# A two-layer transformer tower on one core: the first weight on ScalarE's queue, and small operations, weight turns and final products in another order

## The chip, the cores and the metric

The kernel runs on 1 core of one Trainium2 chip. The metric is the device time of an execution in microseconds (us), the median of several runs.

## The reference

From each of 64 rows of 375 numbers, four overlapping patches of 128 (stride 64) are cut: 256 tokens of 512 features.

```
h = patches @ W.T + b                                # 64 x 4 patches -> 512
h = h + attention0(layernorm(h))                     # 16 heads of 32, over the 4 positions
h = h + experts(layernorm(h))                        # 16 experts of 192, the two best of each token
h = h + attention1(layernorm(h))                     # causal, 16 heads, 4 key/value heads
h = h + ffn1(layernorm(h))                           # 512 -> 2048 -> 512
attention0: activations rounded to 8 bits per token or head, weights to {-1, 0, 1} * mean|W|
ffn1:  x = fwht(x * SU_ug) / 64
       x = silu(x @ W_gate.T * s_g) * (x @ W_up.T * s_u)
       x = fwht(x * SU_dp) / 64
       x = x @ W_down.T * (Wscale_dp * 64)
```

fwht is the Walsh-Hadamard transform over the last axis. Wscale_dp scales each of the 512 output features.

## The kernel before

The 256 tokens lie as two tiles of 128 partitions (`TILES`, index t), and the whole tower runs on them without leaving the core's memory. The program for each engine is written out by hand, in order, and the engines meet only at counting semaphores (`wait_ge`, `then_inc`). An instruction that waits holds up all that stands behind it on its engine. So the order of the lines is the schedule.

**Precision.** Products that need it are done as three: high part by high part, high by low, low by high. ScalarE casts the high part (`main_high`, `rest_high`, `f_high`, `xt_high`, `wd_high`, `u_high`), VectorE subtracts for the low one (`main_low` L1424, `rest_low` L1428, `f_low`, `xt_low`, `wd_low`, `u_low`), TensorE multiplies. Matmuls of plain fp32 take two passes.

**Opening.** SyncE issues every load. The first are the bias row, the patches, the patch weight `tok_w`, then the four weights of the first attention, 1 MB each, into `big_raw` (L373). TensorE makes the embedding (L778). ScalarE sums |W| of a weight (`abs_sum`, L449); TensorE adds that sum over the partitions (`weight_total`, L784); VectorE makes thresholds of it (`weight_scale`, L1202 to L1205); ScalarE turns the weight into two sign matrices (`side`, L460). TensorE multiplies the rounded, transposed tokens (`quantised_transposes` L800) by them (`project`, L790) for queries, keys and values, m = 0, 1, 2. VectorE takes each head's largest value (`largest`, L1264), its scale (`floors`, L1270 and L1272, `head_factors`, `head_steps`) and the rounded heads (`head_round`). `key_products`, a fold, the softmax, and the products with the values follow on VectorE; TensorE sums the latter (L853). Between these, TensorE runs products that nobody reads: `early_warm` (L757) and `warm_up`/`keep_warm` (L750).

**Turns.** The rows of W_down in `down_raw` have to be Hadamard-transformed too. `fold_step` does a part on VectorE; the rest is 16 `turn`s: TensorE multiplies a chunk into a bank (L767, two passes), ScalarE copies it back (`turned_back`, L476). Turns 0 to 7 stand in the first attention, turns 8 to 15 (`TURNS_FIRST` is 8) around the second. `TURN_BANK` says which bank each uses.

**Experts.** 32 units (expert by tile) of three parts each of four products (`unit_products`, L883), one bank of four in turn; `hidden` (L1453) makes silu(gate) * up; `dn` (L723 to L725) multiplies by the down weights of a pair of experts.

**Second attention.** `keys_and_values`, `queries_high`, `queries_low`, `swapped`, then on VectorE `products`, `weights`, `weighted_values`; TensorE sums with `values` (L1027) and multiplies by the output weight.

**Last feed-forward.** 16 chunks f: `ffn_gu(f)` (L1101, L1118), and from f = 7 on `down(f - 7)` behind it. `down(c)` adds chunk c for both tiles to banks 2 and 6. Chunks 12 to 15 are done for tile 0 first, then for tile 1. VectorE multiplies each finished tile by `wsdp` (Wscale_dp; L1790), adds h (L1792), and SyncE stores it in two halves (L412).

## Time and profile before

| | |
|---|---|
| median of 3 runs | 281.83 us (281.79 to 283.18) |
| the profiled execution's own time | 282.39 us |
| its span, first to last instruction | 280.6 us |
| TensorE, matmuls | 264.8 us, 94% of the span |
| VectorE | 227.1 us, 81% |
| ScalarE | 149.4 us, 53% |
| granted TensorE clock, mean | 0.996 |

A matmul's busy time overlaps the next one's, so TensorE at 94% is not TensorE at its peak. A row of the timeline gives start, duration, engine, line, operation, and in brackets how long the engine had been idle before it and what ended that. x4 says that four like instructions were put together. SPq is SyncE's DMA queue.

### The profile page before, as it was taken

How to read it: one execution, taken by the hardware profiler on the slowest of the kernel's cores; microseconds unless marked ns; L12 is line 12 of the kernel's file. 1: busy time of each engine (PE TensorE's matmuls, PEld its weight loads, DVE VectorE, ACT ScalarE, POOL GpSimd, SP SyncE). 2: the span in 40 equal slices, each digit the busy share in tenths (PEclk: the TensorE clock that was granted, in tenths of full speed). 3: DMA queues.
4: the chain of work that ended last, by engine and by line, in shares of the span. 5: the costliest groups of instructions: out<-in, count | busy, mean ns of one | idle time of the engine just before them, and what ended most of it. 6: DMA issues, size and time to landing. Idle time of an engine off the chain costs nothing. (4 is left out here: it accounts for less than half of the span.)

```text
span 280.6 us, 3960 instructions
## 1 busy us (share of the span) xinstructions
PE 264.8 (94%) x1477; PEld 217.6 (78%) x1480; DVE 227.1 (81%) x409; ACT 149.4 (53%) x234; POOL 6.3 (2%) x19
## 2 busy tenths in 40 slices
PE   8779789989999999999999999999999999999993
PEld 3445454658899999989999897766689989999872
DVE  1969999897999988889898676888958894878783
ACT  2798772345563565655555524535466662653530
POOL 0200000000000000000000000000100000000000
PEclk9999999999999999999999999999999999999998
DMA  6960899904244808172630068095000000000003
GB/s 229 427 250 2 290 378 411 446 12 139 86 159 181 306 33 336 23 316 74 262 110 6 0 224 374 2 363 238 0 0 2 0 2 0 0 2 0 2 2 75
DMA packets 6997, 40.43 MB, mean 144 GB/s; under 512 B 1217, under 2 KB 1473, under 8 KB 5314
## 3 DMA queue, kind: packets, MB, share of 16 engines
q1 hardware_dynamic: 6978, 40.18, 37.6%
q8 instruction: 12, 0.20, 0.3%
q14 instruction: 7, 0.06, 0.1%
HBM read 39.13 MB, written 0.52 MB: 141 GB/s over the span
## 5 line engine op out<-in xcount | busy, mean ns | idle before, releaser
L1101 PE MATMUL bank<-s_xf_hi,s_f_hi 128*128 128x256 f32 x128 | 31.2, 282 | 0.5 <-ACT s_xf_hi L675 0.5
L1101 PE MATMUL bank<-s_xf_hi,s_f_lo 128*128 128x256 f32 x128 | 31.1, 281 | 0.0
L543 ACT ACTIVATE s_silu<-bank 128x192 f32<-128x192 f32 x32 | 10.5, 331 | 36.6 <-PE bank L883 32.6
L883 PE MATMUL bank<-s_w_hi,s_xt_hi 128*128 128x384 f32 (+1 forms) x128 | 29.3, 350 | 0.6 <-DVE s_h L1417 0.6
L883 PE MATMUL bank<-s_w_lo,s_xt_hi 128*128 128x384 f32 (+1 forms) x128 | 27.9, 339 | 0.3 <-DVE s_w_lo L1431 0.3
L883 PE MATMUL bank<-s_w_hi,s_xt_lo 128*128 128x384 f32 (+1 forms) x128 | 27.7, 338 | 0.3 <-DVE s_xt_lo L1194 0.3
L1101 PEld LDWEIGHTS bank<-s_xf_hi,s_f_hi 128*128 128x128 f32 x128 | 24.1, 188 | 1.1 <-issue 0.7
L1625 DVE TENSOR_TENSOR s_f_lo<-s_ffn_raw,s_f_hi 128x1024 fp32r<-128x1024 f32 x16 | 19.6, 1225 | 6.0 <-ACT s_f_hi L622 5.9
L1101 PEld LDWEIGHTS bank<-s_xf_hi,s_f_lo 128*128 128x128 f32 x128 | 24.1, 188 | 0.4
L883 PEld LDWEIGHTS bank<-s_w_hi,s_xt_hi 128*128 128x128 f32 x128 | 21.9, 188 | 2.2 <-DVE s_h L1417 0.8
L883 PEld LDWEIGHTS bank<-s_w_lo,s_xt_hi 128*128 128x128 f32 x128 | 22.8, 188 | 0.7 <-DVE s_w_lo L1431 0.7
L883 PEld LDWEIGHTS bank<-s_w_hi,s_xt_lo 128*128 128x128 f32 x128 | 22.8, 188 | 0.5 <-DVE s_xt_lo L1194 0.5
L697 ACT ACTIVATE s_fs<-bank,s_cols 128x256 f32<-128x256 f32 x16 | 7.6, 475 | 26.0 <-PE bank L1118 26.0
L1426 DVE TENSOR_TENSOR s_w_lo<-s_moe_raw,s_w_hi 128x1024 fp32r<-128x1024 f32 x15 | 18.3, 1223 | 3.1 <-ACT s_w_hi L482 3.1
L723 PE MATMUL bank<-s_dn_hi,s_ht_hi 128*128 128x512 f32 x48 | 19.3, 403 | 0.0
L725 PE MATMUL bank<-s_dn_hi,s_ht_lo 128*128 128x512 f32 x48 | 18.8, 392 | 0.0
L724 PE MATMUL bank<-s_dn_lo,s_ht_hi 128*128 128x512 f32 x48 | 18.8, 392 | 0.0
L1118 PE MATMUL bank<-s_xf_lo,s_f_hi 128*128 128x256 f32 x128 | 17.8, 282 | 0.0
L482 ACT CAST s_w_hi<-s_moe_raw 128x1024 fp32r<-128x1024 f32 x16 | 16.7, 1047 | 1.9 <-PE bank L883 1.8
L767 PE MATMUL bank<-s_big_raw,s_con 128*128 128x512 f32 x32 | 15.7, 602 | 1.7 <-DMA s_big_raw<-down_w 1.7
L622 ACT CAST s_f_hi<-s_ffn_raw 128x1024 fp32r<-128x1024 f32 x16 | 16.8, 1050 | 0.2
L1118 PEld LDWEIGHTS bank<-s_xf_lo,s_f_hi 128*128 128x128 f32 x128 | 16.3, 188 | 0.0
(235 smaller groups left out, 559.7 us busy)
## 6 DMA issues: line engine op xcount, KB each, us to landing
s_moe_raw<-moe_gu SPq DMA_DIRECT2D x16, 768.0 KB, 7.2
s_ffn_raw<-ffn_w SPq DMA_DIRECT2D x4, 2048.0 KB, 10.9
s_moe_raw<-moe_dn SPq DMA_DIRECT2D x8, 768.0 KB, 4.4
s_big_raw<-att_w SPq DMA_DIRECT2D x4, 1024.0 KB, 8.9
s_big_raw<-down_w SPq DMA_DIRECT2D x4, 1024.0 KB, 8.0
s_l_raw<-l_w SPq DMA_DIRECT2D x1, 2560.0 KB, 21.1
out<-s_h SPq DMA_DIRECT2D x4, 128.0 KB, 2.3
s_tok_w<-tok_w SPq DMA_DIRECT2D x1, 256.0 KB, 2.6
```

The source lines that it names most:

```text
L482: act.copy(main_part("w_hi", e), main_of(e)).then_inc(guh_ready, 1)
L543: act.activation(B["silu"][i % 2][:], unit_bank(i)[:, 0:F], ACT.Silu).then_inc(silu_done, 1)
L622: act.copy(M["w_hi"][f % 2][:], ffn_chunk_raw(f)).then_inc(fwh_ready, 1)
L723: pe.matmul(dst, x_hi, w_hi, start=first, stop=False)
L724: pe.matmul(dst, x_hi, w_lo, start=False, stop=False)
L725: return pe.matmul(dst, x_lo, w_hi, start=False, stop=last)
L767: pe.matmul(bank[TURN_BANK[i]][:], con[:, K_H:K_H + P], down_raw[:, TURNS[i], :], start=True, stop=True).then_inc(turn_done, 1)
L883: ins = pe.matmul(unit_bank(i)[:, 0:n], xt(k, t)[part % 2], w[:, k, 0:n], start=(first and k == 0), stop=(last and k == KC - 1))
L1101: pe.matmul(tb(j, n)[:, 0:TOK], M[w][j][:, k, n * P:(n + 1) * P], M["xf_hi"][:, k, :], start=(w == "w_hi" and k == 0), stop=False)
L1118: last = pe.matmul(tb(j, n)[:, 0:TOK], M["w_hi"][j][:, k, n * P:(n + 1) * P], M["xf_lo"][:, k, :], start=False, stop=(k == KC - 1))
L1426: dve.tensor_tensor(main_part("w_lo", e), main_of(e), main_part("w_hi", e).bitcast(F32), ALU.subtract)
L1625: dve.tensor_tensor(M["w_lo"][f % 2][:], ffn_chunk_raw(f), M["w_hi"][f % 2][:].bitcast(F32), ALU.subtract).then_inc(fw_ready, 1)
```

## The change

1. **First weight.** `big_raw` for m = 0 is loaded by ScalarE's queue, as its first instruction, and no longer by SyncE's.
2. **First attention.** The five `early_warm(6)` between and behind the projections are gone (30 products), `WARM[0]` is 12 in place of 18. `weight_total(2)` stands between the two `project(0, ., 1)`. On VectorE `floors` of each projection and `weight_scale(2)` stand one wait earlier, the scaling of `sh[:, 5]` is done by ScalarE, and `weight_scale(3)` stands behind the second `key_products`.
3. **Way into the experts.** `rest_low(0)` stands where tile 0's projection is finished, `keep_warm(bank[5], 4)` is gone, unit 0's parts run as 0, 2, 1, and the first part of unit 2 runs before unit 1.
4. **Last expert pair and second attention.** `last_dn` does the four products with the high hidden part first and then the two with the low one. `turn(8)` moves from before them to before `keys_and_values(1)`; turns 9 to 11 stand together before `values(1)`, 12 to 14 before `scaled_transposes(1, ...)`, 15 right before the last feed-forward. `queries_low(0)` stands before `transposes(5)`. ScalarE's and VectorE's counterparts move accordingly.
5. **Last feed-forward.** `down(7)` and `down(8)` run after all 16 `ffn_gu`. The rows of chunks 12 to 15 of W_down are multiplied by `wsdp` on VectorE after f = 7, 8, 11 and 12; these chunks are added up in banks 3 and 7. The sum of chunks 0 to 11 is multiplied by `wsdp` and added to h while TensorE is at the last four, whose sum is then only added. The second half of each stored tile goes by ScalarE's queue.

```diff
-        WARM, GAP, FILL = (18, 24), 20, 7
+        WARM, GAP, FILL = (12, 24), 20, 7
-        TURN_BANK = (3, 7, 5, 3, 7, 3, 7, 3, 5, 1, 5, 1, 5, 0, 4, 0)
+        TURN_BANK = (3, 7, 5, 3, 7, 3, 7, 3, 5, 1, 5, 1, 0, 4, 0, 4)
@@ sync
-            for m in range(4):
+            for m in range(1, 4):
...
             for t in range(TILES):
                 sp.wait_ge(out_ready, t + 1)
-                for j in range(2):
-                    sp.dma_start(by_pos[2 * t + j], h[j * HALF:(j + 1) * HALF, t, :]).then_inc(stored, 16)
+                sp.dma_start(by_pos[2 * t], h[0:HALF, t, :]).then_inc(stored, 16)
@@ scalar
+            act.dma_start(big_raw[:, 0:KC * C], att_w[0]).then_inc(ld_att[0], 16)
...
+            act.wait_ge(g_ready, 1)
+            act.activation(A["sh"][:, 5], A["g3"][:, 0], ACT.Copy, scale=float(D) ** -0.5).then_inc(gx_ready, 1)
...
             f_high(0)
+            q_out(0)
             xt_high(5)
-            q_out(0)
             act.activation(spare1[:], neg_half[:], ACT.Exp)
+            exp(2, L["sc"][:, 2, 0, 0:2], L["sc"][:, 3, 0, 0:2])
             q_out(1)
-            exp(2, L["sc"][:, 2, 0, 0:2], L["sc"][:, 3, 0, 0:2])
+            turned_back(8)
             kv_out(1)
-            turned_back(9)
-            turned_back(10)
...
+                if c >= FC - 4:
+                    act.wait_ge(rows_scaled, c - FC + 5)
...
+            for t in range(TILES):
+                act.wait_ge(out_ready, t + 1)
+                act.dma_start(by_pos[2 * t + 1], h[HALF:P, t, :]).then_inc(stored, 16)
@@ tensor
             project(0, 0, 1)
+            weight_total(2, bank[3][:, 0:1])
             project(0, 1, 1)
-            weight_total(2, bank[3][:, 0:1])
-            early_warm(6, bank[1])
...
+            pe.wait_ge(gu_ready, 1)
             unit_products(0, 0, True, False)
-            keep_warm(bank[5], 4)
+            unit_products(0, 2, False, False)
             pe.wait_ge(xt_ready, 3)
-            unit_products(0, 1, False, False)
+            unit_products(0, 1, False, True)
...
+            unit_products(2, 0, True, False)
             pe.wait_ge(xt_hi_ready, 4)
...
             transposes(4, L["xn"], 0)
-            turn(8)
-            dn(PAIRS - 1, 1, 1, 3)
+            last_dn()
...
             queries_low(1)
+            turn(8)
             keys_and_values(1)
             swapped(1)
...
-            turn(9)
-            turn(10)
             values(0)
...
-            turn(11)
-            turn(12)
+            for i in (9, 10, 11):
+                turn(i)
             values(1)
...
-            for i in range(13, 16):
+            for i in range(12, 15):
                 turn(i)
...
                 lane_transform(j, xt_lo, False).then_inc(xf_done, 1)
+            turn(15)
...
             for f in range(FC):
                 ffn_gu(f)
-                if f >= 7:
+                if 7 <= f < FC - 2:
                     down(f - 7)
-            for c in range(9, FC - 4):
+            for c in range(7, FC - 4):
                 down(c)
@@ vector
+                if f in SCALED_AT:
+                    row = down_raw[:, FC - 4 + SCALED_AT.index(f), :]
+                    if f == SCALED_AT[0]:
+                        dve.wait_ge(turned, FC)
+                    dve.tensor_tensor(row, row, wsdp[:], ALU.mult).then_inc(rows_scaled, 1)
...
+            for t in range(TILES):
+                y = M["u"][:, 2 * t:2 * t + 2, :].rearrange("p a n -> p (a n)")
+                o.mark(dve.tensor_tensor(y, tb(t, 2)[:], wsdp[:], ALU.mult), t)
...
             for t in range(TILES):
                 dve.wait_ge(down_done, FC - 4 + t + 1)
-                if t == 1:
-                    dve.wait_ge(h_kept, 2)
-                y = M["u"][:, 2 * t:2 * t + 2, :].rearrange("p a n -> p (a n)")
-                o.mark(dve.tensor_tensor(y, tb(t, 2)[:], wsdp[:], ALU.mult), t)
                 o.settle(t)
-                dve.tensor_tensor(h[:, t, :], y, h[:, t, :], ALU.add).then_inc(out_ready, 1)
+                dve.tensor_tensor(h[:, t, :], tb(t, 3)[:], h[:, t, :], ALU.add).then_inc(out_ready, 1)
```

VectorE, between the rounded queries (`s_q`) and the first `largest` of the keys; `s_c`, `s_re` are `floors`, `s_sw`, `s_half` are `weight_scale(2)`, `s_g` is `head_steps(0)`. Before:

```order
L1294 TENSOR_TENSOR s_q<-bank,s_f 128x512 x2
L1202 TENSOR_SCALAR s_sw<-bank 128x1
L1204 TENSOR_SCALAR s_half<-s_sw 128x1
L1205 TENSOR_SCALAR s_half<-s_sw 128x1
L1288 SCALAR_TENSOR_TENSOR s_g<-s_am,s_c 128x32
L1270 TENSOR_SCALAR s_c<-s_amax,s_sw 128x2
L1272 RECIPROCAL s_re<-s_c 128x2
L1270 TENSOR_SCALAR s_c<-s_amax,s_sw 128x2
L1272 RECIPROCAL s_re<-s_c 128x2
L1314 TENSOR_SCALAR s_sh<-s_g 128x32
L1264 TENSOR_REDUCE s_am<-bank 128x16 x2
```

The same stretch in the changed kernel:

```order
L1317 TENSOR_TENSOR s_q<-bank,s_f 128x512 x2
L1311 SCALAR_TENSOR_TENSOR s_g<-s_am,s_c 128x32
L1293 TENSOR_SCALAR s_c<-s_amax,s_sw 128x2
L1295 RECIPROCAL s_re<-s_c 128x2
L1287 TENSOR_REDUCE s_am<-bank 128x16 x2
```

Six of eleven rows have left it; five of them stand earlier, and the `s_sh` one is ScalarE's.

TensorE at the end of the last expert pair; L767 is `turn(8)`, L723 to L725 are the products with the down weights. Before:

```order
L717 MATMUL bank<-s_con,s_xn 128x128 x4
L767 MATMUL bank<-s_big_raw,s_con 128x512
L723 MATMUL bank<-s_dn_hi,s_ht_hi 128x512
L724 MATMUL bank<-s_dn_lo,s_ht_hi 128x512
L725 MATMUL bank<-s_dn_hi,s_ht_lo 128x512
```

In the changed kernel:

```order
L726 MATMUL bank<-s_con,s_xn 128x128 x4
L941 MATMUL bank<-s_dn_hi,s_ht_hi 128x512
L941 MATMUL bank<-s_dn_lo,s_ht_hi 128x512
L941 MATMUL bank<-s_dn_hi,s_ht_hi 128x512
L941 MATMUL bank<-s_dn_lo,s_ht_hi 128x512
L944 MATMUL bank<-s_dn_hi,s_ht_lo 128x512 x2
```

The turn is gone from here, and what needs VectorE's low part (`s_ht_lo`) stands last.

## Rows read from the trace of the kernel before

**Rows 1.** Page, busy tenths, TensorE's granted clock and the GB/s moved, in 40 slices of 7 us
```profile
PE   8779789989999999999999999999999999999993
...
PEclk9999999999999999999999999999999999999998
...
GB/s 229 427 250 2 290 378 411 446 12 139 86 159 181 306 33 336 23 316 74 262 110 6 0 224 374 2 363 238 0 0 2 0 2 0 0 2 0 2 2 75
```

**Rows 2.** Timeline, opening: start us, us, engine, line, operation [idle before <- what ended it]
```profile
4.61 3.62 PE L778 MATMUL bank<-s_tok_w,s_z 128*128 128x512 f32 x4
...
10.46 1.91 ACT L449 ACTIVATE s_tern_p<-s_big_raw 128x2048 fp32r<-128x2048 f32 x1 [0.50 <-DMA s_big_raw<-att_w]
...
14.73 1.02 PE L790 MATMUL bank<-s_side,s_qxt 128*128 128x512 bf16 x3 [0.73 <-ACT s_side L460]
...
16.54 1.04 PE L790 MATMUL bank<-s_side,s_qxt 128*128 128x512 bf16 x4 [0.34 <-ACT s_side L460]
...
17.41 0.39 PE L800 MATMUL bank<-s_ident_b,s_qx 128*128 128x128 bf16 x4
...
20.05 0.28 PE L784 MATMUL bank<-s_asum,s_onesf 128*128 128x1 f32 x2
```

**Rows 3.** Timeline, first attention's projections
```profile
22.80 0.15 DVE L1202 TENSOR_SCALAR s_sw<-bank 128x1 f32<-128x1 f32 x1
...
23.21 0.22 DVE L1270 TENSOR_SCALAR s_c<-s_amax,s_sw 128x2 f32<-128x2 f32 x1
...
23.30 2.00 ACT L460 ACTIVATE s_side<-s_big_raw,s_half 128x2048 bf16<-128x2048 f32 x1 [0.90 <-DVE s_half L1205]
...
24.01 0.16 DVE L1314 TENSOR_SCALAR s_sh<-s_g 128x32 f32<-128x32 f32 x1
...
24.29 0.69 DVE L1264 TENSOR_REDUCE s_am<-bank 128x16 f32<-128x512 f32 x1
...
29.92 0.69 DVE L1264 TENSOR_REDUCE s_am<-bank 128x16 f32<-128x512 f32 x1 [0.17 <-PE bank L790]
```

**Rows 4.** Timeline, softmax and weighted values of the first attention
```profile
39.09 0.31 ACT L464 ACTIVATE s_sc<-s_sc 128x128 f32<-128x128 f32 x1 [1.92 <-DVE s_sc L1338]
...
42.48 7.10 PE L853 MATMUL bank<-s_prod,s_con 128*128 128x512 f32 x16 [0.72 <-DVE s_prod L1374]
```

**Rows 5.** Timeline, way into the experts
```profile
54.56 0.69 DVE L1194 TENSOR_TENSOR s_xt_lo<-bank,s_xt_hi 128x512 fp32r<-128x512 f32 x1 [0.77 <-ACT s_xt_hi L470]
...
68.32 1.05 ACT L482 CAST s_w_hi<-s_moe_raw 128x1024 fp32r<-128x1024 f32 x1 [1.22 <-PE bank L883]
```

**Rows 6.** Timeline, last expert pair
```profile
169.91 1.02 PE L767 MATMUL bank<-s_big_raw,s_con 128*128 128x512 f32 x2
```

**Rows 7.** Timeline, second attention
```profile
187.07 0.69 DVE L1194 TENSOR_TENSOR s_xt_lo<-bank,s_xt_hi 128x512 fp32r<-128x512 f32 x1 [1.16 <-ACT s_xt_hi L470]
...
195.28 1.16 PE L1027 MATMUL bank<-s_con,s_prod 128*128 128x128 f32 x8 [0.41 <-DVE s_prod L1691]
```

**Rows 8.** Timeline, first product of the last feed-forward
```profile
206.35 0.36 PE L1101 MATMUL bank<-s_xf_hi,s_f_hi 128*128 128x256 f32 x1 [0.54 <-ACT s_xf_hi L675]
```

**Rows 9.** Timeline, the end
```profile
268.67 0.40 PE L723 MATMUL bank<-s_wd_hi,s_u_hi 128*128 128x512 f32 x1
...
271.24 0.39 PE L725 MATMUL bank<-s_wd_hi,s_u_lo 128*128 128x512 f32 x1
...
275.44 0.40 PE L725 MATMUL bank<-s_wd_hi,s_u_lo 128*128 128x512 f32 x1
275.88 0.69 DVE L1790 TENSOR_TENSOR s_u<-bank,s_wsdp 128x512 f32<-128x512 f32 x1 [1.39 <-PE bank L725]
276.60 0.69 DVE L1792 TENSOR_TENSOR s_h<-s_u,s_h 128x512 f32<-128x512 f32 x1
```

**Rows 10.** One stretch of the last feed-forward: us, PE, PEld, DVE, ACT, POOL busy, clock, DMA, GB/s
```profile
240.00:260.00 20.00, 20.00 (x146) 18.84 (x145) 15.68 (x23) 10.04 (x17) 0.00 (x0) 1.00 0.00 1
```

**Rows 11.** Output stores by line: ns min/median/max of an issue, first and last start
```profile
L412 SPq DMA_DIRECT2D out<-s_h x4: 467/550/598, 274.5 to 277.8; - x4
```

More of the change, by code:

```diff
@@ L1301, in key_products @@
                                   ).then_inc(qk_done, 1)
+            floors(0)
             transposed_out(1)
             largest(0, 0)
-            floors(0)
+            floors(1)
+            weight_scale(2, bank[3][:, 0:1])
             largest(0, 1)
@@ L1342, in _ @@
             key_products(1, A["swapped"][0])
+            weight_scale(3, bank[5][:, 0:1])
             dve.wait_ge(qk_done, 2)
@@ L1404, in _ @@
                 if t == 0:
+                    rest_low(0)
                     xt_low(1)
```

89 lines of the change are left out of this document (52 added, 37 removed).

## The prediction, made before the changed kernel ran

> **What bounds it now.** I read the page's slices first [rows 1]. TensorE stands at 9 tenths in all slices but the first ones and the last, and its granted clock is at the upper of its two levels, 2.4 GHz, until the last slice. So in the middle, from about 75 us to 270 us, time can only be won by taking work or waits from TensorE. The slices before 50 us are different: TensorE is at 7 or 8 there, filler products included. Then I followed the timeline through the five places that the change touches, asking at each which engine the others wait for.
>
> In the **opening**, ScalarE is the gate: it waited 0.50 us for the second weight at 10.46, and TensorE waited 0.73 and 0.34 us for ScalarE's sign matrices before it could transpose tile 1 at 17.41 [rows 2]. From the **projections** to the weighted values VectorE sets the pace: it runs on almost without a gap, while ScalarE waited 0.90 us for a threshold [rows 3] and 1.92 us for the softmax argument, and TensorE 0.72 us for the first weighted value [rows 4]. The first unit of the **experts** is held by a chain over all three engines, and ScalarE waited 1.22 us for unit 1 [rows 5]. At the **last expert pair** a turn stands between TensorE's transposes and the products that VectorE waits for [rows 6]. In the **second attention** the wait goes to and fro, 1.16 us of VectorE and 0.41 us of TensorE [rows 7], then TensorE waits 0.54 us once more [rows 8]. At the **end** TensorE hands over to VectorE, and VectorE to the stores [rows 9, 11]; before that, in the last feed-forward, TensorE is never idle and VectorE has a fifth of its time free [rows 10].
>
> All sums are made against the profiled execution, 282.39 us, 0.56 above the median of 281.83. I carry the difference over to the median.
>
> **1. First weight by ScalarE's queue.** An issue by SyncE takes about half a microsecond [rows 11]. One fewer lets all later loads be issued that much earlier, and the first weight, now behind nothing where it stood behind three issues, leaves earlier by more. The gate is the landing of the second weight, with the same bytes ahead of it: estimate 0.6 us earlier (0.3 to 1.0). Against that, the first weight's 1 MB is now under way together with the patches and `tok_w`, on which the embedding at 4.61 waits. Its delay is not in the trace. Below nothing it can't be, since nothing gets ahead; at most all of the 1 MB goes first, at the 427 GB/s of slice 2 [rows 1] 2.5 us. I take 0.8, a third of that, since both loads share. The embedding's chain has 0.73 + 0.34 = 1.1 us of slack before 17.41, so a delay of 0.8 leaves 0.3 us of gain there. Bounds: +0.8 and, with 1.5 of delay, -0.4.
>
> **2. First attention.** `weight_total(2)` between the two `project(0, ., 1)` delays the last queries by its 0.28 us less overlap [rows 2]: -0.2. On VectorE, between 22.80 and 24.29, stand the threshold (about 0.3), the queries' step (0.1), two `floors` in 24.01 - 23.21 = 0.80, and the scaling of `sh` with its wait, 0.28 [rows 3]. Of these the threshold, one `floors` (0.40) and the scaling go away: +1.0. The threshold and the floors now stand in waits of VectorE before the last queries' `largest`; TensorE's projection covers them. Without that cover they would cost the same again. VectorE twice waited 0.17 us for a projection, one of them at 29.92 [rows 3]. The filler behind each projection goes (30 products), and ScalarE's sign matrices come 0.9 us earlier, so both waits go: +0.34. `weight_scale(3)` moves by one instruction; its start overlaps the product before it: +0.1. It is now late for ScalarE's last two sign matrices, 3.9 us of work (two of 2.00 as at 23.30), but ScalarE then waited 1.92 us for the softmax argument, and loses 1.5 of that at most: nothing. Twelve warm products for eighteen: they end before the first weighted value comes, nothing.
>
> Sum for parts 1 and 2: 0.3 - 0.2 + 1.0 + 0.34 + 0.1 = **1.5 us**, bounds 0.8 and 2.0.
>
> **3. Way into the experts.** `rest_low(0)`, 0.75 us of VectorE, goes into the 0.77 us that VectorE waits before 54.56 [rows 5]: nothing. TensorE does one part of unit 2 (0.7 us) early and drops the filler. But what comes next waits for the first hidden values; these follow from ScalarE's cast at 68.32, that was waiting for unit 1 [rows 5], and unit 1 ends when it did. So TensorE's 0.7 us become a wait. I take 0, bounds 0 and 0.7.
>
> **4. Last expert pair and second attention.** A turn is two passes of 0.43 us, 0.86 us in all (1.02 with its drain at 169.91 [rows 6]). Before 195.28 TensorE carried turns 8 to 12, now 8 to 11: +0.86. TensorE's wait of 0.41 there [rows 7] goes: with the turn away and the low products last, tile 1's sum is ready about 0.8 us earlier, and with `queries_low(0)` first VectorE starts on the scores about 1 us earlier; the 1.16 us that it waited [rows 7] let that through. With `transposes(5)` behind `queries_low(0)`, TensorE gets a new wait for ScalarE's copy, about 0.35 us. Then turn 15 (0.86) is put into a gap of 0.54 [rows 8]: -0.3. Turns 12 to 14 take the place of 13 to 15. Sum 0.86 + 0.41 - 0.35 - 0.3 = **0.6 us**, bounds 0 (the earlier VectorE work is all waited for elsewhere) and 1.2.
>
> **5. End.** The eight steps from 268.67 to 271.24 took 2.57 us, the eighteen from there to 275.44 4.20, or 0.23 each [rows 9]. So 2.57 - 8 x 0.23 = 0.7 us was waiting for VectorE's low parts. With `down(7)` and `down(8)`, twelve products, behind the last `ffn_gu`, TensorE has 2.8 us more work there while VectorE finishes: +0.7. Behind TensorE's last product VectorE multiplied and added, 275.88 to 277.29; only one of two instructions is left: +0.7. The four row scalings of 0.69 us each go to VectorE over some 20 us in which it was free for 20 - 15.68 = 4.3 [rows 10]; nothing, but if they come where `f_low` is due, TensorE waits, at most 0.7 us. The four early operations have TensorE's last 24 products, 5.6 us, as cover. The two stores of tile 1 stood one behind the other, 0.47 to 0.60 us each [rows 11]; now both are issued at once: +0.5. Sum **1.9 us**, bounds 1.2 and 2.1.
>
> By the Trainium skill ("DMA: Bandwidth & Descriptors", "Rules for kernel authors") two transfers to disjoint partition halves serialize on the same engines, and a second issuing engine saves only issue time. If the saving were nothing, the last term would be 0 and the forecast 0.5 us higher; the rows price an issue, so I keep it.
>
> **Sum:** 1.5 + 0 + 0.6 + 1.9 = 4.0 us. Profiled execution 278.4, median **277.8 us**. Ends of the bounds: gains of 2.0 and 6.0, so 279.8 and 275.8.
>
> **Rivals.**
>
> *A. The first weight pushes the embedding out.* Both queues feed the same 16 engines, and if the 1 MB goes ahead of `tok_w`, the embedding is 2.5 us late; less 1.1 of slack, TensorE's transposes come 1.4 us later than before, not 0.3 earlier. Total gain 4.0 - 1.7 = 2.3: **279.5 us**. For it: the first weight would be issued first and has long rows. Against: `tok_w` is small and its packets need only their turn. By the Trainium skill (same page, "Queues, rings and completion order") an engine takes turns between queues, a whole packet at a time; long packets against short ones would land near this rival. Chance 0.2.
>
> *B. The waits are filled, but the chain isn't shortened.* Parts 2 and 4 move small things off VectorE, and the next limit stands close: ScalarE's sign matrices are one long row of work, and TensorE gets three turns in a row before `values(1)`. If part 2 gives half and part 4 nothing, the gain is 0.8 + 0 + 1.6 = 2.4: **279.4 us**. Chance 0.15.
>
> *C. Slower: TensorE falls to its lower clock.* The filler kept it busy. Now its stretch from about 29.5 to 36.7 has long gaps, with the swap product and three turns only. That the granted clock does fall when TensorE stands still shows in the last slice, most of it behind the last product [rows 1, 9]. If it falls here, to 1.2 GHz, and stays there, the sixteen passes of fp32 from 42.48 on, 7.10 / 16 = 0.44 us each [rows 4], take what the embedding's four took in the opening, 3.62 / 4 = 0.91 [rows 2]: 16 x 0.47 = 7.5 us on the path, **285.3 us**. It decides from 4.0 us of loss on, that is from nine slow passes. Against: before, TensorE had gaps of up to 0.7 us here [rows 4] with the clock at 2.4 GHz throughout, and twelve warm products still stand ahead of the passes. Chance 0.06.
>
> *D. More than that.* The unit part of 0.7 counts, and the opening gives its upper bound: **276.2 us**. Chance 0.09.
>
> **Numbers.** My own case has 0.5, 276.8 to 279.0. The range of 276.0 to 280.6 leaves out C and the tails of D, A and B. A measurement of this kernel tells about 0.5%, 1.4 us, from no change: faster means below 280.4. All of the main case and D, nearly all of A and B: 0.86. Within 0.5%: 0.08. Slower: 0.06.
>
> **What would show it.** In the changed profile: the second weight's sum on ScalarE at 9.9 and the embedding at 5.4; no wait of ScalarE before its third pair of sign matrices; the sixteen passes start at 41.0; ScalarE's cast for expert 2 at 66.8; the first product of the last feed-forward at 206.35 - 2.1 = 204.3; steps of 0.23 us up to the last product; one VectorE instruction behind it; two stores at once. TensorE's last product ends at 275.8 - 1.5 - 0.6 - 0.7 = 273.0. It is wrong if the granted clock is below 2.4 GHz between 30 and 50 us, if the sixteen passes start later than 41.7, or if TensorE ends later than 273.9.

## The result, and the profile after

The changed kernel takes **280.55 us** in the median of 20 runs (279.29 to 282.66), the kernel before 281.85 in 20 runs beside it (281.57 to 284.36). The ratio is 0.995, with a 95% interval of 0.9934 to 0.9966: faster by 1.3 us, where 4.0 had been forecast. The profiled execution took 280.39 us, its span is 278.6, against 280.6 for the one before.

Two of the three rows of slices in [rows 1], for the changed kernel (busy tenths and granted clock of TensorE):

```profile
PE   5969589989899999999999999999999999999994
...
PEclk9999979999999999999999999999999999999999
```

Two things differ from before. TensorE's first and fifth slices are emptier (5 tenths each, where 8 and 7 stood), and the granted clock has a 7 in the sixth slice, 35 to 42 us. All of it lies ahead of 50 us. I followed them in the timeline. First the **opening** of the changed kernel, which answers to [rows 2]:

```profile
5.69 1.91 ACT L450 ACTIVATE s_tern_p<-s_big_raw 128x2048 fp32r<-128x2048 f32 x1 [0.79 <-DMA s_big_raw<-att_w]
...
6.04 0.39 DVE L1235 COPY s_z<-s_patches 128x256 f32<-128x256 f32 x1 [5.03 <-DMA s_patches<-patches]
...
7.34 3.78 PE L787 MATMUL bank<-s_tok_w,s_z 128*128 128x512 f32 x4 [2.53 <-DMA s_tok_w<-tok_w]
...
9.89 1.91 ACT L450 ACTIVATE s_tern_p<-s_big_raw 128x2048 fp32r<-128x2048 f32 x1 [2.19 <-DMA s_big_raw<-att_w]
...
14.00 3.90 ACT L461 ACTIVATE s_side<-s_big_raw,s_half 128x2048 bf16<-128x2048 f32 x2 [2.10 <-DVE s_half L1228]
...
19.15 0.39 PE L809 MATMUL bank<-s_ident_b,s_qx 128*128 128x128 bf16 x4
```

The first weight's megabyte has landed by 5.69, before the 128 KB of patches, though `tok_w` and the patches were issued within 0.8 us of it. The embedding starts at 7.34 instead of 4.61, 2.73 us late. (Of the profiled executions that follow, three more have this load on ScalarE's queue: the embedding starts at 6.68, 6.75 and 7.17. The ten with it on SyncE's queue, the kernel before among them, have 4.60 to 5.20.) The second weight's sum stands at 9.89, where I had said 9.9. But ScalarE then waits 2.10 us for the threshold that it needs for the sign matrices: `weight_scale(0)` is behind the embedding's layer norm on VectorE, and that is late. The transposes of tile 1 come at 19.15, not 17.41.

Then the stretch before the **sixteen passes**, timeline and stretches of 2 us (columns: length; busy time and instructions of PE, PEld, DVE, ACT, POOL; granted clock; share and GB/s of the DMA engines):

```profile
33.05 0.43 PE L838 MATMUL bank<-s_g,s_swap_f 128*128 128x64 f32 x2 [1.75 <-DVE s_g L1311]
...
35.87 4.39 PE L776 MATMUL bank<-s_big_raw,s_con 128*128 128x512 f32 x6 [2.38 <-DMA s_big_raw<-down_w]
...
41.32 1.23 DVE L1395 TENSOR_TENSOR s_prod<-s_v,s_sc 128x1024 f32<-128x1024 int16 x1
41.63 1.78 PE L759 MATMUL bank<-s_had 128*128 128x256 f32 x12
...
43.10 1.23 DVE L1395 TENSOR_TENSOR s_prod<-s_v_swapped,s_sc 128x1024 f32<-128x1024 int16 x1 [0.55 <-DMA s_v_swapped<-s_v]
43.26 1.02 PE L859 MATMUL bank<-s_prod,s_con 128*128 128x512 f32 x2
...
50.60 1.02 PE L776 MATMUL bank<-s_big_raw,s_con 128*128 128x512 f32 x2
```
```profile
32.00:34.00 2.00, 0.43 (x2) 0.30 (x2) 2.00 (x4) 0.46 (x2) 0.00 (x0) 1.00 0.98 401
34.00:36.00 2.00, 0.13 (x1) 0.16 (x1) 1.93 (x6) 1.52 (x1) 0.00 (x0) 0.91 1.04 434
36.00:38.00 2.00, 2.00 (x3) 0.96 (x4) 1.97 (x2) 2.00 (x2) 0.00 (x0) 0.50 1.03 365
38.00:40.00 2.00, 2.00 (x4) 0.66 (x4) 1.52 (x6) 1.06 (x3) 0.00 (x0) 0.74 0.97 368
```

TensorE stood idle for 1.75 us and, after the swap product, for 2.38 us. Then the clock goes to half, 1.2 GHz, and the three turns run six passes in 4.39 us. [Rows 4] had the whole stretch at 2.4 GHz. VectorE starts the first weighted values at 41.32, almost as before (41.11). Before, the passes followed that start by 1.37 us (42.48 [rows 4]), so here they could have begun at 42.69. They begin at 43.26, with no wait in front of them: 0.57 us is TensorE's own lateness. (Right ahead of them TensorE runs the twelve warm products of `WARM[0]`, 1.78 us of filler from 41.63 on. Whether the passes would begin in time without these wasn't tried.)

VectorE is late in this stretch too, and for another reason. It makes the weighted values in four products, and the second needs `s_v_swapped`, the values as a DMA on SyncE's queue has exchanged them. VectorE waits 0.55 us for that transfer at 43.10. The kernel before has no wait there:

```profile
42.25 1.22 DVE L1374 TENSOR_TENSOR s_prod<-s_v_swapped,s_sc 128x1024 f32<-128x1024 int16 x1
...
49.86 1.02 PE L767 MATMUL bank<-s_big_raw,s_con 128*128 128x512 f32 x2
```

The last row of each is the turn that TensorE runs behind the sixteen passes. From the first weighted value to that turn it is 50.60 - 41.32 = 9.28 us, and was 49.86 - 41.11 = 8.75. So 0.53 us is lost here, as much as VectorE's wait alone would take. TensorE's lateness lies beside that wait, not on top of it.

From that turn on the difference to the kernel before stays at 0.68 to 0.74 us up to the last expert pair. In the **second attention** it turns:

```profile
177.64 0.50 PE L739 MATMUL bank<-s_w_hi,s_xt_hi 128*128 128x512 f32 x1 [0.29 <-ACT s_xt_hi L471]
...
193.15 2.84 PE L1050 MATMUL bank<-s_con,s_prod 128*128 128x128 f32 x24
...
205.79 0.43 PE L1122 MATMUL bank<-s_xf_hi,s_f_hi 128*128 128x256 f32 x1
```

The three groups of eight value products run as one, without the 0.41 us of [rows 7], and the first product of the last feed-forward starts 0.56 us before that of [rows 8]. At the **end**, which answers to [rows 9]:

```profile
274.21 0.40 PE L734 MATMUL bank<-s_wd_hi,s_u_lo 128*128 128x512 f32 x1
274.65 0.69 DVE L1824 TENSOR_TENSOR s_h<-bank,s_h 128x512 f32<-128x512 f32 x1 [1.25 <-PE bank L734]
275.37 0.49 SPq L413 DMA_DIRECT2D out<-s_h  x1
275.37 0.49 ACTq L717 DMA_DIRECT2D out<-s_h  x1
```

From the feed-forward's first product to the end of TensorE's last one it is 274.61 - 205.79 = 68.82 us, and was 275.84 - 206.35 = 69.49: 0.67 less. Behind the last product stands 278.6 - 274.61 = 3.99 us, and was 4.76: 0.77 less.

### The profile page after: what moved, and what is told of

Same layout as the page of the kernel before. It is cut to its first block, busy times and chain, and to the rows that moved or that the text cites. A ratio compares the mean times of both kernels' runs of the same rounds, so it can differ in the third digit from the quotient of the medians.

```text
span 278.6 us, 3892 instructions
## 1 busy us (share of the span) xinstructions
PE 261.0 (94%) x1438; PEld 213.6 (77%) x1440; DVE 230.0 (83%) x414; ACT 149.5 (54%) x235; POOL 7.0 (2%) x19
## 3 DMA queue, kind: packets, MB, share of 16 engines
q10 hardware_dynamic: 304, 1.31, 1.3%
## 4 chain that ended last, share of the span: by engine, by line
PE 80%; DVE 10%; DMA 4%; ACT 2%; issue 1%; SPq 1%; POOL 0%; ACTq 0%; DVEq 0%; POOLq 0%
PE bank L889 23%; PE bank L1122 10%; PE bank L732 7%; PE bank L734 6%; PE bank L733 6%; PE bank L1139 5%; PE bank L776 4%; PE bank L859 2%; DMA s_big_raw<-down_w 2%; DMA s_tok_w<-tok_w 2%; PE bank L915 2%; PE bank L745 2%; PE bank L1050 2%; PE bank L799 1%; PE bank L739 1%
## 5 line engine op out<-in xcount | busy, mean ns | idle before, releaser
L776 PE MATMUL bank<-s_big_raw,s_con 128*128 128x512 f32 x32 | 17.1, 655 | 2.4 <-DMA s_big_raw<-down_w 2.4
L732 PE MATMUL bank<-s_dn_hi,s_ht_hi 128*128 128x512 f32 x46 | 18.1, 395 | 0.0
L733 PE MATMUL bank<-s_dn_lo,s_ht_hi 128*128 128x512 f32 x46 | 18.0, 392 | 0.0
L734 PE MATMUL bank<-s_dn_hi,s_ht_lo 128*128 128x512 f32 x46 | 18.0, 392 | 0.0
```

The lines of the kernel that those rows point to most:

```text
L732: pe.matmul(dst, x_hi, w_hi, start=first, stop=False)
L733: pe.matmul(dst, x_hi, w_lo, start=False, stop=False)
L734: return pe.matmul(dst, x_lo, w_hi, start=False, stop=last)
L776: pe.matmul(bank[TURN_BANK[i]][:], con[:, K_H:K_H + P], down_raw[:, TURNS[i], :], start=True, stop=True).then_inc(turn_done, 1)
```

## The experiments

Two causes were to be told apart from each other and from "the gain wasn't there": the late opening (theory 1), and the fall of the clock in front of the sixteen passes (theory 2). VectorE's wait for the exchanged values was no theory when these kernels were chosen; their traces are read for it below. Each kernel is given in the median, beside runs of the kernel before on the same chip, with the ratio to these and its interval.

### The first weight's queue alone, on the kernel before

```diff
-            for m in range(4):
+            for m in range(1, 4):
...
+            act.dma_start(big_raw[:, 0:KC * C], att_w[0]).then_inc(ld_att[0], 16)
             act.wait_ge(bias_done, 1)
```

> The kernel before, with nothing changed but the queue of the first weight. Theory 1 (the 1 MB goes ahead of the patches and tok_w, and that sets the opening): the embedding starts at about 7.3 us as in the changed kernel (4.61 before), the transposes of tile 1 at about 19.1 (17.41 before), and the kernel is 1 to 1.8 us slower than before. Rival (the opening's delay is covered by slack, and the changed kernel lost its time elsewhere): embedding late all the same, but at most 0.4 us slower than before.

Measured: 283.51 us beside 282.0, ratio 1.0051 (1.0033 to 1.0069). Theory 1 holds. Timeline of this kernel:

```profile
7.17 3.78 PE L779 MATMUL bank<-s_tok_w,s_z 128*128 128x512 f32 x4 [2.36 <-DMA s_tok_w<-tok_w]
...
9.67 1.91 ACT L449 ACTIVATE s_tern_p<-s_big_raw 128x2048 fp32r<-128x2048 f32 x1 [1.60 <-DMA s_big_raw<-att_w]
...
13.82 3.90 ACT L460 ACTIVATE s_side<-s_big_raw,s_half 128x2048 bf16<-128x2048 f32 x2 [2.15 <-DVE s_half L1206]
...
18.98 0.39 PE L801 MATMUL bank<-s_ident_b,s_qx 128*128 128x128 bf16 x4
...
35.79 4.51 PE L768 MATMUL bank<-s_big_raw,s_con 128*128 128x512 f32 x6 [1.09 <-DMA s_big_raw<-down_w]
```

The weight's part is there, and so are the wait for the threshold and the late transposes. The edit that I had priced at a gain of 0.3 us costs 1.5. The last row holds something that theory 2 had not said: the turns are mostly at half speed here too, 4.51 us for six passes, with every filler product in place. Here that costs nothing behind it: the passes follow the first weighted value (42.65) by 1.37 us again, and the turn behind them by 8.75.

### The first weight back on SyncE's queue, in the changed kernel

The diff is the reverse of the one above.

> The changed kernel with the first weight back on SyncE's queue. Theory 1: embedding at 4.6 us, transposes of tile 1 at about 17.4, the 1.7 us come back in full up to the first projections, and the kernel is 1 to 2 us faster than the changed one, near 279. Theory 2 (what is lost is lost where the granted clock falls, at 36 to 39 us in the changed kernel, whatever the opening does): the clock falls here too, and no more than 0.5 us comes back, 280 to 280.5.

Measured: 279.64 us beside 282.0, ratio 0.9905 (0.9883 to 0.9927), 0.9 us under the changed kernel. The opening comes back in full, and nearly half of it is lost again:

```profile
4.60 3.62 PE L786 MATMUL bank<-s_tok_w,s_z 128*128 128x512 f32 x4
...
16.88 0.39 PE L808 MATMUL bank<-s_ident_b,s_qx 128*128 128x128 bf16 x4
...
33.20 5.46 PE L775 MATMUL bank<-s_big_raw,s_con 128*128 128x512 f32 x6 [1.67 <-DMA s_big_raw<-down_w]
...
42.04 3.16 PE L858 MATMUL bank<-s_prod,s_con 128*128 128x512 f32 x7
```

The transposes are 2.27 us earlier than in the changed kernel, the sixteen passes only 1.22. All six passes of the turns are at the lower clock, 5.46 us, and so are the first products behind them. VectorE starts the weighted values at 39.36, so by the distance of 1.37 the passes could begin at 40.73, and they are 1.31 us late. VectorE has no wait for the exchanged values in this execution. So theory 1 holds, and here the fall of the clock takes back part of what the opening gives.

### Filler put back, in two places

In the changed kernel, the 30 filler products behind the projections again (`early_warm(6, bank[1])` at each):

> The changed kernel with the 30 filler products behind the projections put back, the rest as changed. Theory 2 (the fillers' absence lets the clock fall): no stretch below 2.4 GHz between 30 and 50 us, the three turns at 0.43 us a pass and not 0.86, sixteen passes at about 42.0 to 42.5, runs that lie as close together as those of the kernel before, and 0.8 to 1.5 us faster than the changed kernel in the median. Theory 1 alone: the clock is no cause, the kernel stays at 280.5 or gets up to 0.5 us slower by the fillers.

Measured: 281.83 us beside 282.0, ratio 0.9975 (0.9953 to 0.9998), 1.3 us over the changed kernel. Both expectations fail. Six of the twelve runs are at a clock of 0.982 to 0.988 with 282.28 to 284.08 us: these products don't hold the clock. The other six, at 0.992 to 0.997, took 280.60 to 281.38, some 0.9 us more than the runs of the changed kernel at 0.992 to 0.994 (median 279.95): these products lie on TensorE's path. Stretches of the profiled execution, the slowest of the twelve (columns as above):

```profile
18.00:21.00 3.00, 2.55 (x11) 1.13 (x9) 1.21 (x8) 2.88 (x3) 0.00 (x0) 0.61 0.01 2
...
36.00:38.00 2.00, 0.00 (x0) 0.00 (x0) 1.94 (x5) 1.25 (x2) 0.00 (x0) 0.85 1.03 426
38.00:40.00 2.00, 1.85 (x3) 0.85 (x4) 1.99 (x1) 2.00 (x2) 0.00 (x0) 0.50 1.00 360
```

It falls twice in this execution: behind a wait of 2.40 us in the opening, and behind the idle 2.26 us before the turns, although TensorE was busy with filler until 0.71 us before the swap product.

So the filler was put where TensorE was idle, and nowhere else:

```diff
-            early_warm(12, bank[1])
+            early_warm(24, bank[1])
             pe.wait_ge(g_ready, 3)
...
+            pe.wait_ge(k16_ready, TILES)
+            early_warm(16, bank[6])
             pe.wait_ge(v16_ready, TILES)
             turn(0)
```

> The changed kernel with filler only where TensorE stood idle: 24 instead of 12 small products behind the third weight's total, and 16 behind the swap product, where it waited 2.38 us for the down weights. Theory 2: the clock stays at 2.4 GHz, the turns take 0.43 us a pass, 0.8 to 1.5 us faster in the median and less scatter; if it was the fillers behind the projections that held the clock, the clock falls here all the same and the time stays at 280.5. Theory 1 alone: no change.

Measured: 279.89 us beside 282.0, ratio 0.9911 (0.9887 to 0.9935), 0.7 us under the changed kernel, whose interval begins where this one ends. In the profiled execution the clock is at 2.4 GHz in every stretch from 12 to 44 us:

```profile
32.73 1.91 PE L766 MATMUL bank<-s_onesf 128*128 128x256 bf16 x16
...
35.31 1.96 PE L776 MATMUL bank<-s_big_raw,s_con 128*128 128x512 f32 x4 [0.67 <-DMA s_big_raw<-down_w]
```

The passes start at 42.09, where VectorE's pace allows them (40.72 + 1.37). But the turn behind them stands 9.23 us after the first weighted value, for 9.28 in the changed kernel: VectorE still waits, 0.51 us, for the exchanged values. So the 0.57 us read above do not come back in this trace. The 0.6 us by which its span is shorter are already there in the opening, with the transposes of tile 1 at 18.56 for 19.15.

What the filler changes shows in the mean granted clock of all runs. None of the 20 runs of the changed kernel is above 0.994: ten at 0.992 to 0.994 with a median of 279.95 us, five at 0.988 with 281.07, five at 0.981 or 0.982 with 281.95. Some 1 us for each step, and that is the scatter. Here five of six runs are at 0.996 to 1.0, within 279.31 to 279.99, no faster than the upper group there, and the one at 0.994 took 281.23. So the lower median comes from the runs at 0.988 and below, which are half of the changed kernel's and none of these six. The profiled execution of the changed kernel (0.993) is not one of them.

### Both repairs, and the queues of the stores

The changed kernel with the first weight on SyncE's queue and the filler of the last diff:

> The changed kernel with both repairs: the first weight on SyncE's queue, and filler where TensorE stood idle (24 small products for 12, and 16 behind the swap product). If the two losses are separate, the gains add, 0.9 + 0.7 = 1.6 us: 279.0 in the median or a little under, clock 1.0 throughout, embedding at 4.6, sixteen passes at about 40.8. If the earlier opening is lost again at the next wait (down weights, VectorE), the time stays at 279.6 to 279.9, where each repair alone stands.

Measured: **278.38 us** beside 281.97, ratio 0.9887 (0.9865 to 0.9908). The gains add and more (2.2 us for 1.6), and both kernels are beaten. Timeline:

```profile
4.99 3.78 PE L786 MATMUL bank<-s_tok_w,s_z 128*128 128x512 f32 x4 [0.17 <-DMA s_tok_w<-tok_w]
...
33.95 1.96 PE L775 MATMUL bank<-s_big_raw,s_con 128*128 128x512 f32 x4 [0.62 <-DMA s_big_raw<-down_w]
...
39.41 1.22 DVE L1396 TENSOR_TENSOR s_prod<-s_v,s_sc 128x1024 f32<-128x1024 int16 x1
40.78 4.53 PE L860 MATMUL bank<-s_prod,s_con 128*128 128x512 f32 x10
41.11 1.23 DVE L1396 TENSOR_TENSOR s_prod<-s_v_swapped,s_sc 128x1024 f32<-128x1024 int16 x1 [0.48 <-DMA s_v_swapped<-s_v]
...
48.62 1.02 PE L775 MATMUL bank<-s_big_raw,s_con 128*128 128x512 f32 x2
```

The passes start at 40.78, where VectorE's pace allows them (39.41 + 1.37). With the clock held, the first weight's queue is worth 278.0 - 276.7 = 1.3 us of span, 1.5 in the medians, what it cost in the kernel before.

VectorE's wait is still there, 0.48 us. With all eight executions side by side, it can be told from the clock (us; the last two columns count from VectorE's first weighted value):

| profiled execution | six passes of the turns | VectorE's wait for the exchanged values | the passes start | the turn behind them |
|---|---|---|---|---|
| kernel before | 1.95 + 1.10 | none | 1.37 | 8.75 |
| before, first weight's queue | 4.51 | none | 1.37 | 8.75 |
| before, part 2 alone | 4.48 | 0.28 | 1.99 | 9.29 |
| changed kernel | 4.39 | 0.55 | 1.94 | 9.28 |
| changed, filler where idle | 1.96 + 1.10 | 0.51 | 1.37 | 9.23 |
| both repairs | 1.96 + 1.10 | 0.48 | 1.37 | 9.21 |
| both repairs, patches by ScalarE | 1.88 + 1.10 | none | 1.37 | 8.75 |
| changed, weight back on SyncE's queue | 5.46 | none | 2.68 | 9.98 |

With the wait and the clock held, some 0.5 us is lost; with the wait and turns of 4.4 us, no more than 0.08 on top of that; with neither, nothing. Only where all six passes are slow does the clock cost much, 1.23 us. The exchange is late where it lands 9.4 to 9.6 us after its issue (the slower of its two halves) and not where it lands after 7.4 to 8.0. The loads of the down weights ahead of it on the same queue go with it, 9.3 to 9.5 us in the median against 8.0 or 8.1. Why they take longer isn't known, and no run changed the place of this transfer.

In the kernel with both repairs the stores were put back on one queue:

```diff
-                sp.dma_start(by_pos[2 * t], h[0:HALF, t, :]).then_inc(stored, 16)
+                for j in range(2):
+                    sp.dma_start(by_pos[2 * t + j], h[j * HALF:(j + 1) * HALF, t, :]).then_inc(stored, 16)
```

> The same kernel with both stores of a tile on SyncE's queue, one behind the other, and nothing else changed. By the prediction's last term: 0.5 us slower, the last store issued half a microsecond later (467 to 598 ns each) and landing that much later. Rival (the transfers go through the same 16 engines one after the other, so an earlier issue only waits in the queue): within 0.1 us of it.

Measured: 278.77 us beside 281.97, ratio 0.99 (0.9884 to 0.9916). The median is 0.39 us higher, but the intervals overlap, and four of the five runs had a clock of 0.993 or 0.994, as only one of the other kernel's six had. In the profiled one it fell in the opening: the transposes of tile 1 are at 18.47 for 16.93. So I read the trace behind VectorE's last instruction. It starts at 273.90 here and ends the span at 277.9, 4.0 us later; with two queues:

```profile
272.36 0.40 PE L733 MATMUL bank<-s_wd_hi,s_u_lo 128*128 128x512 f32 x1
272.80 0.69 DVE L1825 TENSOR_TENSOR s_h<-bank,s_h 128x512 f32<-128x512 f32 x1 [1.26 <-PE bank L733]
```

The span is 276.7, so 3.9 us. The second queue is worth 0.1 us, not 0.5. The issues did start at once, but the stores on ScalarE's queue took longer to land, 2.8 us in the median against 2.3 before. DMA view of the changed kernel's end (KB each, us from issue to landing):

```profile
out<-s_h SPq DMA_DIRECT2D x2, 128.0 KB, 2.3
out<-s_h ACTq DMA_DIRECT2D x2, 128.0 KB, 2.8
```

By the trace the rival was right. In the prediction the Trainium skill ("DMA: Bandwidth & Descriptors", "Rules for kernel authors") stood against this term; by that rule two transfers to disjoint halves serialize, and the trace agrees, with 0.1 us between the two ends.

### Parts 5, 4, 2 and 3 alone, on the kernel before

Each of these kernels has the lines of one part of the change and no others. Part 5 (also the row scaling, and the four early operations):

```diff
-                if f >= 7:
+                if 7 <= f < FC - 2:
...
-                dve.tensor_tensor(h[:, t, :], y, h[:, t, :], ALU.add).then_inc(out_ready, 1)
+                dve.tensor_tensor(h[:, t, :], tb(t, 3)[:], h[:, t, :], ALU.add).then_inc(out_ready, 1)
```

> The kernel before with part 5 alone (rows scaled early, two down steps moved behind the last feed-forward step, one VectorE instruction behind the last product, two output queues). Forecast on record for this part: 1.9 us. By the trace of the changed kernel: TensorE's last product ends 0.71 us earlier against its own feed-forward loop, and what follows it is 0.77 us shorter, 1.5 us together, so 280.4 to 280.6. Rival (the scaled rows hold up the low parts in the loop, and their cost is hidden by another part's gain): 1.0 us or less.

Measured: 280.53 us beside 281.97, ratio 0.9957 (0.9939 to 0.9974): 1.4 us, as the trace of the changed kernel has it. The last lines repeat its end, TensorE at 274.29 and one VectorE instruction at 274.73, 0.44 us behind. The scaled rows hold nothing up that shows.

Part 4 (also `TURN_BANK`, ScalarE's order, and `xt_low(5)` behind the first products):

```diff
-            turn(8)
-            dn(PAIRS - 1, 1, 1, 3)
+            last_dn()
...
-            pe.wait_ge(turned, 9)
+            queries_low(0)
             transposes(5, L["xn"], 1)
-            queries_low(0)
             swapped(0)
             queries_high(1)
             queries_low(1)
+            turn(8)
```

> The kernel before with part 4 alone (a turn out of the last expert pair, the order in the second attention, the turns' places). Forecast on record: 0.6 us. By the shift between 166 and 206 us in the changed kernel, from +0.7 to -0.56, it gives 1.2 us, so 280.7. Rival (part of that shift came from the later start that the parts before gave, a wait that was there anyway and swallowed the delay): 0.6 us or less, 281.3.

Measured: 280.70 us beside 281.97, ratio 0.9961 (0.9949 to 0.9974): 1.3 us, twice the forecast. The rival falls: this kernel begins its passes at 41.92 and the last feed-forward at 204.56, 162.64 us, for 163.87 before, with no part ahead of it changed.

```profile
204.56 0.44 PE L1111 MATMUL bank<-s_xf_hi,s_f_hi 128*128 128x256 f32 x1
```

Part 2 (also the filler behind each projection out, and the scaling of `sh` on ScalarE):

```diff
+            floors(0)
             transposed_out(1)
             largest(0, 0)
-            floors(0)
+            floors(1)
+            weight_scale(2, bank[3][:, 0:1])
             largest(0, 1)
```

> The kernel before with part 2 alone (order of the small operations in the first attention, filler behind the projections gone, twelve warm products for eighteen); the first weight stays on SyncE's queue. Forecast on record for this part: 1.2 us. By the kernel with both repairs, which starts its sixteen passes 1.7 us before the kernel before did (40.78 against 42.48) with the filler put where TensorE was idle: 1.2 to 1.7 us if the clock holds. Theory 2: the clock falls at the turns here too, part of the gain is lost, 281.0 to 281.5, and the runs scatter as those of the changed kernel do.

Measured: 281.71 us beside 282.16, ratio 0.9983 (0.9962 to 1.0003), 280.8 to 282.89: the interval just reaches 1. Six of the twelve runs are at a clock of 0.994 with 280.80 to 281.82 us, six at 0.977 to 0.989 with 281.07 to 282.89. The profiled one is of the first group, and its turns are slow:

```profile
33.91 4.48 PE L769 MATMUL bank<-s_big_raw,s_con 128*128 128x512 f32 x6 [2.34 <-DMA s_big_raw<-down_w]
...
39.41 1.22 DVE L1371 TENSOR_TENSOR s_prod<-s_v,s_sc 128x1024 f32<-128x1024 int16 x1
...
41.40 4.02 PE L852 MATMUL bank<-s_prod,s_con 128*128 128x512 f32 x9
```

On VectorE, from the first `largest` (17.69 here, 18.18 before) to the first weighted value (39.41, and 41.11) it is 21.72 for 22.93 us: 1.21 us gained, the 1.2 of the forecast. The passes start at 41.40, not at 40.78, and VectorE waits 0.28 us for the exchanged values. By the turn behind the passes 9.29 - 8.75 = 0.54 us of it is lost.

Part 3 (also `rest_low(0)` in VectorE's wait):

```diff
             unit_products(0, 0, True, False)
-            keep_warm(bank[5], 4)
+            unit_products(0, 2, False, False)
...
+            unit_products(2, 0, True, False)
```

> The kernel before with part 3 alone (the first unit's products and unit 2's first part ahead). Forecast on record: nothing, with 0 to 0.7. What is left of the kernel with both repairs after parts 4 and 5 (1.27 and 1.44 measured alone) and a part 2 of 1.2 is a loss or gain of at most 0.3, so 281.7 to 282.2. Rival (TensorE's earlier part of unit 2 comes through): 281.3.

Measured: 282.84 us beside 282.16, ratio 1.0013 (0.999 to 1.0036), 281.55 to 284.23. No gain, as forecast; a small loss is neither shown nor excluded. Part 3 drops four filler products, and five of the twelve runs are above 283, four of these at a clock of 0.987. Whether the one follows from the other wasn't tried.

### Two more questions

The kernel before, with filler in TensorE's idle stretches:

```diff
-            early_warm(12, bank[1])
+            early_warm(16, bank[1])
             pe.wait_ge(g_ready, 3)
...
+            pe.wait_ge(k16_ready, TILES)
+            early_warm(8, bank[6])
             pe.wait_ge(v16_ready, TILES)
```

> The kernel before with more filler in TensorE's two idle stretches only, 16 for 12 behind the third weight's total and 8 behind the swap product. Theory 2 (the clock's fall ahead of the sixteen passes makes the upper half of the kernel before's own runs, 282.9 to 283.4): clock 0.998 to 1.0 in nearly all runs, median 281.7, no run above 282.5. Rival (the scatter of the kernel before has another source): the same median, 282.0, and some third of the runs still near 283.

Measured: 282.53 us beside 282.16, ratio 0.9998 (0.998 to 1.0017), 281.68 to 283.43. My expectation fails. Six of twelve runs are at a clock of 0.997 to 1.0 with 281.68 to 282.31 us, six at 0.992 to 0.994 with 282.75 to 283.43. The time goes with the clock, but filler at this place doesn't keep it up in the kernel before. The profiled run has no fall, so where it falls in the others isn't shown. That it can fall in the opening is, by the 0.61 from 18 to 21 us above and by the kernel with one store queue.

The kernel with both repairs, and the patches by ScalarE's queue:

```diff
-            sp.dma_start(A["patches"][:], patches).then_inc(ld_in, 16)
...
+            act.dma_start(A["patches"][:], patches).then_inc(ld_in, 16)
             act.wait_ge(bias_done, 1)
```

> The kernel with both repairs (278.38), but the patches' load, 128 KB, issued by ScalarE's queue. One issue fewer on SyncE's queue, as in the change, and no megabyte beside tok_w. If an issue saved is worth what it takes where loads do not push each other out, tok_w and all the weights come 0.37 to 0.4 us earlier, the second weight's sum starts at 9.6 and the kernel gains 0.2 to 0.4 us. Rival (the 16 engines are the limit from 2 us on and the bytes ahead of the second weight are the same): 0.1 us or nothing, the second weight's sum at 9.9.

Measured: 278.52 us beside 282.16, ratio 0.9858 (0.9833 to 0.9883). The interval overlaps with that of the kernel it was taken from, and the medians are alike. The timeline has the mechanism:

```profile
9.49 1.92 ACT L449 ACTIVATE s_tern_p<-s_big_raw 128x2048 fp32r<-128x2048 f32 x1 [0.49 <-DMA s_big_raw<-att_w]
...
40.30 4.10 PE L860 MATMUL bank<-s_prod,s_con 128*128 128x512 f32 x9 [0.85 <-DVE s_prod L1396]
```

The second weight's sum is 0.49 us earlier (9.98 there), and the passes are 0.48 earlier. In the nine profiled executions with all loads on SyncE's queue that sum starts at 9.71 to 10.46, so this one is ahead of them all; how much of it is owed to the issue taken off that queue can't be told from one execution. The embedding isn't held up (4.88), since what goes by the other queue is 128 KB and not 1 MB. The other half of the 0.9 us by which the span is shorter (275.8 for 276.7) is VectorE's wait for the exchanged values, which this execution doesn't have. Its best run, 277.6 us, is the fastest of all; that it is faster in the median isn't shown.

## Why the prediction was wrong, by its steps

Alone, the five parts give, by their ratios to the kernel before (times 282, plus is slower): part 1 +1.4 us, part 2 -0.5, part 3 +0.4, part 4 -1.1, part 5 -1.2, together -1.0. Forecast were -0.3, -1.2, 0, -0.6 and -1.9. All of them together gave -1.4 by the same measure. Each of these has an interval of 0.4 to 0.7 us to either side, so within that the parts are additive, and they can be held against the terms.

**Part 1** is the step that failed most: "I take 0.8, a third of that, since both loads share." The embedding was 2.73 us late in the changed kernel and 2.07 to 2.56 in the three other executions, about the bound of 2.5 that stood for "all of the 1 MB goes first". The part was to gain 0.3 and cost 1.4 to 1.5, and that is most of what is missing.

The slack of 1.1 us that I subtracted is right against the profile that it was read from (2.73 late, and 19.15 - 17.41 = 1.74 at the transposes: 1.0). But the opening of that execution was itself late, about by what its own time stood above the median (0.56): its second weight's sum is at 10.46, those of the eight others with all loads on SyncE's queue at 9.71 to 10.22. With part 1 alone the embedding is 2.56 us later than before, and the transposes 2.10 us later than the 16.88 of the kernel with the weight back, so the slack was 0.5. TensorE's two waits for the sign matrices were 0.21 + 0.34 there.

The 0.6 us that the second weight was to come earlier were in part there: 9.25 to 9.89 in the four executions, 0.46 by the medians of the two groups. They were worth nothing, since ScalarE then waits for the threshold, which hangs on the embedding through VectorE's queue; the sum had no such wait. Rival A had the mechanism, at a chance of 0.2.

Why the megabyte goes ahead can be worked out in part. In the changed kernel's DMA view of the first 14 us, ScalarE's queue moved it in few packets:

```profile
q10 hardware_dynamic: 144, 1.05, 21.1%
```

That is 7.3 KB a packet. `tok_w` has rows of 512 fp32, 2 KB, and the patches 1 KB. If an engine serves both queues packet by packet, several kilobytes of weight pass for each 1 or 2 KB on the other side, and the weight is through first. By the Trainium skill ("DMA: Bandwidth & Descriptors", "Queues, rings and completion order") the turns are by whole packets. The order of landing fits that (weight by 5.69, patches by 6.04, `tok_w` by 7.34), but it doesn't show it: that the profile counts the same packets isn't known, and no run here changed their size. So that the megabyte goes ahead is shown, and why is argued.

**Part 2** was right on VectorE up to the first weighted value, 1.21 us for 1.24, and wrong in what follows: the sum lets all of it through. By the turn behind the sixteen passes 0.53 us is lost in the changed kernel and 0.54 with part 2 alone. Two things went wrong there at once.

One is in no term and no rival: the transfer that exchanges the values. It landed up to 2 us later after its issue than before (9.6 for 7.6), and VectorE waited 0.28 to 0.55 us for it in the four executions with this wait in the table. Where it didn't (both repairs, patches by ScalarE), the distance was back to 8.75.

The other is "Twelve warm products for eighteen: they end before the first weighted value comes, nothing". TensorE reaches them later. The sum had six passes at 0.43 us, and they took 0.73 to 0.91. Rival C named this stretch, at 0.06, but as a loss on the sixteen passes. The clock was up again when they ran; the loss is in the turns ahead of them, and the sixteen passes start 0.57 to 1.31 us late, where the rival had 7.5. In the profiled execution of the changed kernel this is hidden beside VectorE's wait. In the runs at a mean clock of 0.988 and 0.981 it is not, if they lose their 1 and 2 us here; none of those of the changed kernel was profiled, but the kernel with the weight back was, at 0.988, and there it cost 1.23 us. The removed fillers between the projections were not the cause, as their return shows. What stands in front of the turns is idle time, 1.75 and 2.38 us with the swap product between them, where it was 0.72 and 1.11; with filler there none of 22 runs of four kernels has a mean clock below 0.993, where 14 of the 26 runs of the changed kernel, as it is and with the weight back, stand at 0.988 or below.

**Part 3**, nothing: right as far as the runs tell.

**Part 4** was 1.2 for 0.6. The turn, the wait of 0.41 and the new wait (0.29 for my 0.35) are about as priced, 0.98 in sum. The term that failed is turn 15: "put into a gap of 0.54: -0.3". It cost nothing that shows. At 205.08 it runs while ScalarE casts, and the first product follows it at once. Some 0.2 us of the 1.23 stay unassigned.

**Part 5** was 1.4 for 1.9. The low parts' waits gave 0.67 for 0.7, one VectorE instruction fewer 0.7, the second queue 0.07 to 0.1 for 0.5: "now both are issued at once: +0.5" is the term that failed, since the earlier issue did not bring an earlier landing.

Two of the rivals' sums don't follow from their terms: B takes 1.6 for part 5, whose term is 1.9, and what D adds (0.7, and 0.5 in the opening) gives 276.6, not 276.2.

Of the signs in the last paragraph these came as said: the second weight's sum at 9.9, no wait of ScalarE before its third pair of sign matrices, steps of 0.23 us to the end, one VectorE instruction and two stores at once behind it. The embedding (7.34 for 5.4), the passes (43.26 for 41.0), the cast for expert 2 (69.05 for 66.8), the last feed-forward (205.79 for 204.3) and TensorE's last product (274.61 for 273.0) did not. The three that were to prove me wrong all did: a clock below 2.4 GHz between 30 and 50 us, passes later than 41.7 (43.26), TensorE ending later than 273.9 (274.61). The time lies inside the range by 0.05 us only.

## What to carry to other kernels

Moving a load to a second queue changes what it is served beside: ask not only what an issue costs, but which small load the rest waits for, and send small loads, not the largest, by the free queue. Filler in the idle stretch itself, right in front of slow work, kept the clock from its deepest falls in the changed kernel and did nothing that shows in the kernel before; on the path it cost 0.9 us and did not hold the clock at all. A gain on the pacing engine is worth what the others can follow, so look for when each arrives, at the clock it will then have, and the transfers too. And where two are late by the same half microsecond, mending one gives nothing: read what the next common instruction did, not only the one that was mended.

## What the runs showed that I had not expected

The transfer that exchanges the values took up to 2 us longer in the kernels with part 2 than in any other (9.6 us for 7.6), but not in all executions, and it hid what the clock did in the same stretch.

TensorE's clock fell to half for single stretches of a few microseconds (0.91, 0.50 and 0.74 over 2 us each in the changed kernel), in some executions of a kernel and not in others: a wait of 1.09 us in front of the turns had it fall in one kernel, one of 1.11 in the kernel before had not. The mean clock of a run and its time go together by about 1 us a step. Which execution is hit, and by how much, stays open.
